# First-layer TensorE loop unrolled over 16 tiles, node updates 5, 5 and 6 tiles apart

## The reference

```python
edge_index = jnp.stack([src, dst])
# layer 0, typed: Q, K, V from the node plus 0.1 * query_emb, four heads of 64
mod_k = K[src] + 0.2 * rel_w[edge_relations][:, None, :]
scores = jnp.einsum('ehd,ehd->eh', Q[dst], mod_k) / D ** 0.5
w = softmax of scores over the edges of one dst
agg = jax.ops.segment_sum(w[:, :, None] * V[src], dst, num_segments=N)
msgs = jnp.where(deg[:, None, None] > 0, agg, V)
x = layernorm(msgs.reshape(N, H * D) @ Wo + bo + node_features) * gamma + beta
x1 = layernorm(node_features + x)
# layer 1, plain: xp = x1 @ W, each node is an edge to itself as well
alpha = leaky_relu(a_src[src] + a_dst[dst], 0.2)
agg = segment_sum(xp[src] * softmax(alpha over dst), dst)
out = layernorm(x1 + elu(agg + bias))
```

## Time and profile before

| | |
|---|---|
| time, median of 3 runs | 4471.25 us (4469.44 to 4473.03) |
| span of the profiled execution | 6181.0 us, 164,556 instructions |
| busy share of the span: PE, PEld, DVE, ACT, POOL | 69%, 44%, 53%, 42%, 49% |
| granted TensorE clock, mean | 0.790 of full speed |
| DMA | 1,055.91 MB, mean 171 GB/s |

### The profile page before, as it was taken

One profiled execution on the slowest core, in us unless ns is written; L12 is line 12 of the kernel. 1 busy time (PEld: TensorE's weight loads), 2 busy tenths in 40 slices (PEclk: granted clock), 3 DMA queues, 4 the chain that ended last, 5 costly groups with the idle time before them and its releaser, 6 DMA issues. The chain is left out here.

```text
span 6181.0 us, 164556 instructions
## 1 busy us (share of the span) xinstructions
PE 4261.5 (69%) x50798; PEld 2746.6 (44%) x50798; DVE 3295.8 (53%) x10527; ACT 2576.2 (42%) x6781; POOL 3049.7 (49%) x3229
## 2 busy tenths in 40 slices
PE   7958878777778787778786555555555555555554
PEld 4634444444444444444443444444444443444443
DVE  3235555555555555555554455555555555555555
ACT  2323344444444444444343444444444444444444
POOL 1245555545555555555452555555555555555553
PEclk9989999999999999999997666656566566565666
DMA  7856676666666666666664555555555555555554
GB/s 224 282 163 191 185 189 186 186 186 185 186 187 183 186 186 187 185 186 186 184 185 114 145 153 156 152 151 153 152 153 153 150 152 149 154 152 152 154 150 123
DMA packets 820553, 1055.91 MB, mean 171 GB/s; under 512 B 458633, under 2 KB 632338, under 8 KB 820464
## 3 DMA queue, kind: packets, MB, share of 16 engines
q0 software_dynamic: 225072, 730.03, 42.9%
q1 hardware_dynamic: 594078, 324.02, 20.6%
q10 hardware_dynamic: 1314, 0.99, 0.1%
HBM read 919.46 MB, written 133.59 MB: 170 GB/s over the span
## 5 line engine op out<-in xcount | busy, mean ns | idle before, releaser
L766 POOL DMA_INDIRECT typed_rows<-kv,typed_index x1563 | 1491.3, 954 | 1470.8 <-remote 570.5
L1298 POOL DMA_INDIRECT plain_rows<-xp,plain_index x1563 | 1486.0, 951 | 1359.5 <-remote 536.1
L875 PE MATMUL typed_p_s<-typed_kt,typed_q 64*32 64x416 f32 x4168 | 835.7, 549 | 336.6 <-issue 289.7
L997 DVE CUSTOM_DVE_ANT_0 typed_weight<-typed_p_s,typed_far 128x416 f32<-128x416 f32 x521 | 308.3, 592 | 1113.6 <-PE typed_p_s L875 1080.8
L1400 PE MATMUL plain_p_o<-plain_rows,plain_weight_t 128*32 128x65 f32 x16672 | 630.5, 296 | 331.5 <-issue 310.7
L1433 DVE SCALAR_TENSOR_TENSOR plain_p_s<-plain_p_s,plain_a_dst,plain_damped 128x416 f32<-128x416 f32 x521 | 342.3, 657 | 865.9 <-ACT plain_damped L1553 475.1
L1389 PE MATMUL plain_p_s<-all_cst,plain_rows 128*128 128x128 f32 x2084 | 546.2, 395 | 346.0 <-issue 319.6
L1375 PE MATMUL plain_p_w<-all_cst,plain_weight 128*128 128x128 f32 x1563 | 437.5, 404 | 431.6 <-issue 286.0
L1400 PEld LDWEIGHTS plain_p_o<-plain_rows,plain_weight_t 128*32 128x32 f32 x16672 | 459.2, 154 | 556.6 <-issue 516.7
L1167 ACT ACTIVATE typed_weight<-typed_weight,typed_col 128x416 f32<-128x416 f32 x521 | 334.7, 642 | 806.6 <-issue 549.7
L1389 PEld LDWEIGHTS plain_p_s<-all_cst,plain_rows 128*128 128x128 f32 x2084 | 406.0, 210 | 463.6 <-issue 437.6
(11 more groups left out here) (191 smaller groups left out, 6936.5 us busy)
## 6 DMA issues: line engine op xcount, KB each, us to landing
typed_match<-match SPq DMA_DIRECT2D x131, 208.0 KB
plain_match<-match SPq DMA_DIRECT2D x131, 208.0 KB
agg<-qkv_zero SPq DMA_DIRECT2D x98, 264.0 KB
typed_agg<-agg SPq DMA_DIRECT2D x98, 264.0 KB
plain_agg<-agg SPq DMA_DIRECT2D x98, 264.0 KB
kv<-qkv_kv SPq DMA_DIRECT2D x98, 258.0 KB
typed_kinds<-match SPq DMA_DIRECT2D x131, 192.0 KB
typed_rows<-kv,typed_index POOLq DMA_INDIRECT x1563
```

What stands on the lines that cost most here:

```text
L766: pool.indirect_dma_start(rows[:, r, j, :], None, k.kv, bass.IndirectOffsetOnAxis(ap=index[:, g, at:at + 1], axis=0)).then_inc(rows_in[r], 16)
L875: last = pe.matmul(p_s[at:at + TN, 0:SLOTS], q[own, m, :, h // 2], kt[own, h // 2, lo:lo + SLOTS], start=True, stop=True, tile_position=(H ...
L1298: pool.indirect_dma_start(rows[:, r, j, :], None, k.xp, bass.IndirectOffsetOnAxis(ap=index[:, g, at:at + 1], axis=0)).then_inc(rows_in[r], 16)
```

## The change

The places of blocks become 5, 5 and 6 tiles apart in all engines and both layers (GAP 5). TensorE's first-layer loop becomes one loop over 16 tiles after 41 tiles written out. Update and projection are placed by `BlockPart`s: the update at shift 1, ahead of the aggregation, the projection at shift 3 for all three, between score and relate. Before, the projections of the two halves stood at the start of step place + 3 and the third right behind its update. Nothing that is computed changes.

```diff
-GAP = 4
+GAP = 5
...
-    PE_FIRST = 9
+    PE_FIRST = 41
...
-            def step(t, copied=None):
-                for part in (TilePart(TURN_LAG, turn_weights), TilePart(LAG, lambda b: aggregate(b, copied)), TilePart(SCORE, score),
-                             TilePart(0, relate), TilePart(KEY, arrive)):
-                    part.at(t)
+            done = [0]
+
+            def next_update(b):
+                update(b.n, done[0])
+
+            def next_move(b):
+                move(b.n)
+
+            updates = BlockPart(1, -1, next_update, ROWS + PROJECT)
+            moves = BlockPart(3, -1, next_move, ROWS + PROJECT)
+
+            def step(t):
+                copied = None
+                TilePart(TURN_LAG, turn_weights).at(t)
+                place = t.c - 1 - POS
+                if place % PERIOD in (0, GAP, 2 * GAP) and t.c >= 0:
+                    b = Step(t.q, GROUP * (place // PERIOD) + place % PERIOD // GAP, GROUP).back(-1)
+                    if b.c >= 0:
+                        done[0] = t.n
+                        updates.at(t)
+                        copied = b.n + 2
+                TilePart(LAG, lambda b: aggregate(b, copied)).at(t)
+                TilePart(SCORE, score).at(t)
+                moves.at(t)
+                TilePart(0, relate).at(t)
+                TilePart(KEY, arrive).at(t)
 
             pe.wait_ge(setup, 1)
             for n in range(PE_FIRST):
-                step(Step(0, n, HALF))
+                step(Step(0, n, PERIOD))
             with pe.Fori(0, (TILES - PE_FIRST) // PERIOD) as q_:
-                with pe.Fori(0, 2) as half:
-                    for c in range(PE_FIRST, PE_FIRST + HALF):
...
-                        if c == PE_FIRST + GAP:
-                            update(q_ * GROUP + half, q_ * PERIOD + half * HALF + c)
-                            copied = q_ * GROUP + half + 2
-                        if c == PE_FIRST + GAP + 2:
-                            move(q_ * GROUP + half)
-                        step(Step(q_ * 2 + half, c, HALF), copied)
-                update(q_ * GROUP + 2, q_ * PERIOD + PERIOD + PE_FIRST)
-                move(q_ * GROUP + 2)
-            v = (TILES - PE_FIRST) // PERIOD * GROUP
+                for c in range(PE_FIRST, PE_FIRST + PERIOD):
+                    step(Step(q_, c, PERIOD))
             for n in range(TILES, TILES + LAG):
...
+                step(Step(0, n, PERIOD))
+            last = TILES + LAG - 1
+            updated = 1 + sum(block_place(b) + 1 <= last for b in range(ROWS))
+            moved_on = 1 + sum(block_place(b) + 3 <= last for b in range(ROWS))
+            for v in range(moved_on, updated):
+                move(v)
+            for v in range(updated, ROWS + PROJECT):
                 update(v, TILES, True)
                 move(v)
```

## The result

The changed kernel takes 4764.69 us (median, 4761.07 to 4769.10) beside 4470.70 us (4469.44 to 4473.03) for the kernel before on the same chip: 1.066 times, with a 95% interval of 1.0647 to 1.0674. It is 294 us slower, far above the 4511 forecast and the range's upper end of 4565.

A forecast was written before the change was run, and what follows sets the result against it. The prediction took GpSimd's gathers to set most of the timed time (4,382 of 4471 us). Its terms, +52 - 5 + 0 - 10 + 3 = +40 us, gave 4511 us, range 4415 to 4565.

The forecast's parts named there:

- the price of the jump: TensorE's first-layer loop: 3.37 us a fetch less 1.5 covered, 1.8 exposed at 29 jumps, +52 us (bounds 0 to 98).
- the 16-tile body: TensorE's first-layer loop: about 1,880 instructions, 7.5 packets, taken as fetched anew rather than kept, at +52 us.
- The cover: At TensorE's loop branch: its sequencer runs ahead of its array, so 1.5 us of queued work hides part of the fetch.
- rival (3): At the loop's jumps: cover gone, by an empty queue or slower fetch; 98 us, 4557 or somewhat more; chance 0.14.
- The first layer's places: Updates and projections in the first layer: -5 us from shorter x1 waits, 0 (bounds -20 and +30) for the projection's place.
- The wait on the copied message: First layer, ahead of TensorE's aggregation: 105.8 us of waits on the copied turned message, said to stay.
- The second layer: VectorE's steps there become more even: 45 to 88 us gained if VectorE sets the pace, nothing if GpSimd does; taken -10.
- the covered end: Second layer: the end of the gain's range where GpSimd's gathers set the pace and nothing is gained; 10 taken near it.
- The end of layer one: Behind the first layer's last tile: one update more falls there, 13 and not 12, +3 us.
- The floor: Whole kernel: 3,126 gathers at 1.246 us plus 487 us around them, 4,382 us, 89 under the timed kernel; ceiling for gain.
- rival (2): First layer: code is fetched, but GpSimd sets the pace and its slack hides the stall; 4459 to 4475 us; chance 0.14.
- What was to show it: Trace signs: 220 to 240 q8 packets or none, branch 3 or 0.2 us, longer step behind, update steps 6.4 to 7.

The follow-up runs named there:

- e2: Changed kernel with eight spare bias matmuls ahead of TensorE's first tile, shifting the loop's start to just behind a code packet's start: 4562.17 us, 1.0204 of before.
- e8: Changed kernel with 64 spare narrow matmuls ahead of the first tile, leaving some 139 instructions of the loop's first packet ahead: 4602.64 us, 1.0289 of before.
- e7: Kernel before with TensorE's second-layer loop over 16 tiles, not 8 (some 1,375 instructions, 5.4 packets): 4472.82 us, 0.9997 of before.
- e3: Changed kernel with TensorE's first-layer loop over 160 tiles and 3 passes, 2 jumps back and not 29: 4498.27 us, 1.0065 of before.
- e4: As e3, but updates 4 tiles apart in all engines as before: 4502.82 us, 1.0075 of before.
- e5: Changed kernel with TensorE's first layer written out over all 521 tiles, no loop: 4501.28 us, 1.0061 of before.
- e6: As e5, but each projection ahead of turn_weights, not between score and relate: 4478.99 us, 1.0010 of before.
- e9: As e3 over 240 tiles and 2 passes, with e2's eight spare matmuls and e6's place of the projection: 4469.48 us, 0.9999 of before.
- e1: Kernel before, unedited, profiled a second time: profiled execution 4471.4 us, timed 4475.07 us.
- e10: As e7 with 8 spare narrow matmuls a tile in that loop, some 1,885 instructions a pass: 4476.36 us, timed once.

## Why the prediction was wrong

**The step that failed is the price of the jump.** That the 16-tile body would not be kept was right (290 packets in 29 passes), and the branch itself was nearly so: 3.8 us in the median where the earlier trace rows had 3.37, the low end of the 3.36 to 4.49 that this one jump takes in the profiles of all runs. The cover was right as well: at 1217.27 the work queued reaches to 1218.78, 1.5 us. What the cover leaves is a wait of 2.6 us (75.8 / 29 in e2), not 1.8; that a jump at full clock costs 2.0 us net, near the 1.8, is in part luck, since the steps around it make up for the rest. What failed is the sentence that this branch "has a row": it was taken for the whole price. The row is that of a jump at 6177.6 us with hardly any code to run behind it, so a second fetch could not show in it. Measured, a jump costs 9.70 us:

| part of the 29 jumps | predicted | measured |
|---|---|---|
| wait for the target's packet | 52 | 77 (L860's waits) |
| wait for the next packet | not seen | 156 (L889's waits) |
| the rest: lower clock, restart of the engines behind | not seen | 281 - 77 - 156 = 48 |

The second line hangs on where the loop's first instruction happens to lie in its packet: e8 has 22 us in that place, e2 half a microsecond. With it gone (e2) the change costs 92 us: above the 52 for the fetch because the wait is longer and the clock falls at every second jump (14 x 2.0 + 15 x 4.0 = 88), and near the 98 us of rival (3), though not by its mechanism: the cover is there. On which of the two sides a kernel falls hangs on the number of instructions ahead of its loop, which the diff alone doesn't show.

The Trainium skill (Runtime: NRT & Kernel Launch, Instruction fetch mechanics) gives TensorE's memory 2048 instructions in blocks of 256 and lets a taken branch out of the current two pages wait for a fetch. The runs fit the 2048 if blocks touched in part and the one fetched ahead are counted: 1,375 instructions touch at most 7 blocks and are kept, while 1,885 that begin some 5 behind the start of a block (e2) touch 8 and are fetched anew, 9 packets a pass; beginning 10 ahead of its end they touch 9, and 10 packets come (the changed kernel, 290 / 29). They don't fit the two pages: e7 jumps back 5.4 packets in 0.22 us.

**The first layer's places**, -5 + 0 predicted: some +7 of the 288 us are not the jumps. Without jumps the spacing gives 4.5 us over both layers (e3, e4), about what was put, and the place between score and relate, costed at nothing within -20 and +30, takes 15 to 22 (e5 against e6; e3 against e9, less the 14 us by which their jumps differ). The wait on the copied message (L1186) did not shrink: 63 us against 47. What the prediction said of the place, that the next score comes later either way, is where it erred: behind one projection of three it matters on which side it stands.

**The second layer**, -10 predicted: +5 measured, which is not clear of scatter (from first to last gather 1963.2 to 1972.8 us in the profiles with the new spacing, 1962.6 in e4 and 1968.2 in e1 with the old one). VectorE's steps did become even, as said: in 464 intervals between lower bounds 70 were over 5 us in e1 and 24 after the change. It bought nothing that shows, since the gathers set the pace there; the covered end was the right one.

**The end of layer one**, +3: the handover and the end grew by 1.4 and 1.2.

**The floor** of 4,382 us, gathers at their own spacing plus what lies around: no run came under it. e1's period is 62.4 us with 59.8 us of gathers in it, and the 2.6 us left are what the gathers wait for TensorE (2.6 x 32.5 = 84.5 us, the row has 84.7). So in the first layer the steps set the pace and not the gathers, and some 85 us were to be had there, of which e9 took 2.5. This is also why rival (2) failed where it stood: gathers that wait already give a stall of TensorE no slack, and even in e2 2.0 of the 2.6 us come on top. In the second layer the same rival is true (e10).

**What was to show it**: the branch at 3 us, the longer step behind it and q8 through the whole loop came as foretold. The 220 to 240 packets were 290, and that surplus was the sign: 7.4 packets of code, but 10 fetched a pass, two ends touched in part and a packet ahead that the jump throws away. The steps with an update are even, but not at 6.4 to 7 us, which were read from a stretched execution: from one start of L843 to the next they are 4.89 and 4.91 in the median and, behind the jump, 5.66; in e1 they are 4.46, 5.36 and 5.20.

## What to carry to other kernels

Before a loop of TensorE is unrolled, count its instructions, and in a trace, not in the source (one spare f32 matmul was four): here 1,375 were kept and 1,885 were not, and a jump into code that isn't kept costs 2 to 4 us where work lies behind the target and 10 where the target's packet ends at once. Ask not only how long the branch takes but what is fetched next, and how much work there is until then; a few idle instructions ahead of the loop moved this kernel by 200 us. Whether a stall counts is settled by the stage: a jump cost 10 us in a layer whose gathers wait for TensorE, and next to nothing in one whose TensorE waits for rows.

## What the runs showed of the hardware

- Behind a jump the next packet is not there in time by itself: in the changed kernel TensorE went on 6.7 us after the branch had ended (1221.44 to 1228.17), with 10 instructions in between; 139 instructions hid most of this (e8), some 250 all of it (e2).
- With the DMA engines at a share of 0.82 in that loop the branch takes 3.8 us in the median, the jump at the end, behind the last gather, takes 3.37 in the earlier trace rows and 3.36 to 4.49 over all runs: the load of the transfers makes little of its length.
- With the changed kernel's two gaps (2.92 and 5.45 us at 1217) the granted clock fell at all 29 jumps; with the one gap of some 2.6 us that is left in e2 it fell at 15 of them, and each of those cost 2 us more (4.0 against 2.0).
- Straight code over 521 tiles, no jump in it, ran 13 us behind the same code in a loop of three passes without its two jumps (63.00 against 62.58 us in 16 tiles).
- One profiled execution of the kernel before was 1.38 times as long as its timed runs, in both loops; a second was not. A floor worked out from rows (here the gathers' own spacing) stands against that; step lengths don't.
